# Projections, attention and output moved into one block, with single buffers and five projection banks

## The reference

```python
x = x + xattn(layernorm(x), ctx)      # 16 heads of 32, masked softmax, Wq Wk Wv Wo with biases
x = x + ffn(layernorm(x))             # fake-quantised: w_gate, w_up (1408 x 512), w_down (512 x 1408)
```

## Time and profile before

| what | value |
|---|---|
| median of three runs | 1161.38 us (1160.01 to 1163.06) |
| the profiled execution | 1157.98 us, span 1156.2 us |
| PE busy, share of the span | 92% |
| DVE, POOL, ACT busy | 66%, 55%, 44% |
| DMA queue q1 | 217.12 MB, 68.0% of 16 engines' span |
| mean granted clock of TensorE | 0.95 of full speed |

### The profile page before, as it was taken

One profiled execution on the slowest core, in us unless ns is written; L12 is line 12 of the kernel. 1 busy time (PEld: TensorE's weight loads), 2 busy tenths in 40 slices (PEclk: granted clock), 3 DMA queues, 4 the chain that ended last, 5 costly groups with the idle time before them and its releaser, 6 DMA issues. The chain is left out here.

```text
span 1156.2 us, 18186 instructions
## 1 busy us (share of the span) xinstructions
PE 1064.3 (92%) x6550; PEld 704.7 (61%) x6550; DVE 764.6 (66%) x1315; ACT 512.8 (44%) x881; POOL 630.3 (55%) x346
## 2 busy tenths in 40 slices
PE   5999999999629989999999999899995799998898
PEld 4888888888516656666666666456663344443343
DVE  5665456654329757777777777138989477877785
ACT  3322223222102657666766677641110555553553
POOL 3433455334440979999999999555434113100373
PEclk9999999999855989999999999899997799999899
DMA  6987677856699897678887774448997353100876
GB/s 205 315 266 238 212 271 255 274 167 198 203 189 189 186 233 159 149 179 177 183 185 170 160 181 115 109 137 220 286 281 190 96 224 122 36 1 2 319 243 218
DMA packets 129619, 218.08 MB, mean 189 GB/s; under 512 B 29320, under 2 KB 55688, under 8 KB 128330
## 3 DMA queue, kind: packets, MB, share of 16 engines
q1 hardware_dynamic: 129546, 217.12, 68.0%
...
## 5 line engine op out<-in xcount | busy, mean ns | idle before, releaser
L783 ACT ACTIVATE a_probs<-a_banks 128x512 f32<-128x512 f32 (+2 forms) x512 | 233.8, 535 | 128.9 <-PE a_banks L991 101.7
L718 POOL TENSOR_TENSOR a_pair_sums<-a_probs,a_probs 128x2048 f32<-128x2048 f32 x48 | 222.1, 4626 | 65.2 <-ACT a_probs L783 57.4
L858 DVE TENSOR_REDUCE a_max<-a_banks 128x2 f32<-128x512 f32 x192 | 123.2, 684 | 52.9 <-PE a_banks L962 52.7
L991 PE MATMUL a_banks<-a_queries,a_keys 97*128 97x512 f32 x384 | 147.8, 428 | 9.1 <-ACT a_probs L783 6.0
L962 PE MATMUL a_banks<-a_keys,a_queries 96*128 96x256 f32 x384 | 86.1, 320 | 32.1 <-DMA a_queries<-q_split 32.1
L967 PE MATMUL a_banks<-a_keys,a_queries 96*128 96x512 f32 (+1 forms) x256 | 115.2, 464 | 0.0
L854 DVE CUSTOM_DVE_ANT_0 a_masked_scores<-a_banks,kept_mask 128x384 f32<-128x384 f32 (+1 forms) x128 | 79.5, 621 | 49.2 <-PE a_banks L967 48.9
L858 DVE TENSOR_REDUCE a_max_parts<-a_banks 128x1 f32<-128x512 f32 x128 | 87.9, 687 | 25.1 <-PE a_banks L967 21.9
L962 PEld LDWEIGHTS a_banks<-a_keys,a_queries 96*128 96x128 f32 x384 | 70.4, 206 | 53.8 <-DMA a_queries<-q_split 32.8
L1347 POOL TENSOR_TENSOR d_out<-d_out,f_x 128x512 f32<-128x512 f32 x28 | 42.6, 1547 | 99.1 <-DVE d_out L1375 99.1
L1231 DVE SCALAR_TENSOR_TENSOR f_h<-g_up,kept_up_scales,f_h 128x512 f32<-128x512 f32 (+1 forms) x88 | 64.2, 746 | 47.2 <-ACT f_h L1196 35.4
...
## 6 DMA issues: line engine op xcount, KB each, us to landing
...
```

Of the source, the lines that this page charges most:

```text
L718: pool.tensor_tensor(PP[u % 2], PR[2 * c % 4], PR[(2 * c + 1) % 4], ALU.add).then_inc(paired, 1)
L783: act.activation(PR[kt % 4][:, j, 0:w], STB[:, n % NST, 0:w], ACT.Exp, scale=SCALE).then_inc(edone, 1)
L858: dve.tensor_reduce(out, src, AX.X, ALU.max).then_inc(wfree, 1)
L991: op = pe.matmul(out.rearrange("p (c t) -> p c t", t=SIT), keys, q, start=True, stop=True)
```

## The change

Projections, attention and output become one block. SBUF is laid out anew: buffers of the projections lie over the stacks of attention and over its probabilities and pair sums. To make room, x, context, their turned forms, and the stages of K and Q exist once or half as often (two stages for four uses a step), and the V stage holds one item in place of two. The projections keep five banks (NB = 5, PB), three serve the score pieces. Loops now run over steps 0 to 3 (EARLY = 4), steps 4 to 7 are written out.

SP loads stack 0 in step 4, stack 1 in step 5, stacks 2 and 3 and the first values in step 7, between the other transfers. The x of the next chunk is loaded after XTURN has freed x, and DVE takes its moments after the third K item and the rest of the layernorm after the fourth. The raw weights are loaded after the second V store of their own step, behind the same wait `fst`. All 56 pieces of groups 0 and 1 run two by two behind the Q and V items from the Q items of step 4 on. Eight pieces of group 2 (FIRST) come right after the first transposed scores. POOL's first pair waits for all stores of K and Q. The weights quantised last are stored from within group 0, and values 1 to 3 loaded after that.

```diff
+FIRST = 8
+S_FIRST = (2, 2, 3, 3, 3, 3, 2, 2)
...
-        NB = 8
         CHAIN_LN = 7
         HI = 4 * KT
-        TAIL = [(BATCH - 1, u) for u in range(2)]
+        TAIL = [(n // 2, n % 2) for n in range(EARLY, NCH)]
+        PB = (0, 1, 2, 6, 7)
...
-            def step(b, u, tail, final):
+            sp.wait_ge(free, NB + KT)
+            load_c(1)
+
+            def step(b, u):
                 n = 2 * b + u
-                for i in range(2):
-                    s.reach(sp, free, NB + at(n) + VALUE + 2 * i + 2)
-                    d = vs.rearrange("(n t p) c -> n p t c", t=TT, p=P)[n][:, 2 * i:2 * i + 2, :]
-                    sp.dma_start(d, VST[i][:]).then_inc(vout[i], 16)
-                if not tail:
+                late = n - EARLY if isinstance(n, int) else None
+                if late == 0:
+                    for q in sout:
+                        sp.wait_ge(q, 32 * 5)
+                for t in range(TT):
+                    s.reach(sp, free, NB + at(n) + VALUE + t + 1)
+                    sp.dma_start(vs.rearrange("(n t p) c -> n p t c", t=TT, p=P)[n][:, t, :], VST[t % 2]).then_inc(vout[t % 2], 16)
+                    if late in (0, 1):
+                        A.load_stack(sp, late, t)
+                    if t == 1:
+                        s.reach(sp, fst, 32 * (n + 1))
+                        ffn_load(n, u, b)
+                if more(n, 1):
                     s.reach(sp, free, NB + at(n) + XTURN + KT)
-                    load_c(n + 2, u)
-                    load_x(n + 2, u)
-                for i in range(4):
-                    item = KEY + 2 * i if i < 2 else query(final) + 2 * (i - 2)
-                    s.reach(sp, free, NB + at(n) + item + 2)
-                    dst = (ks, ks, qs, qs)[i]
-                    for part in range(2):
-                        d = dst[part].rearrange("(m p) t -> p m t", p=P)[:, 2 * (i % 2):2 * (i % 2) + 2, bass.ds(n * CH, CH)]
-                        sp.dma_start(d, f32(STG[i][part][:])).then_inc(sout[i], 16)
-                s.reach(sp, fq, n + 1)
-                d = gu_q[u].rearrange("(b p j) n -> b p j n", p=FP, j=FJ)[b]
-                sp.dma_start(d, FQ[:]).then_inc(fst, 16)
-                sp.dma_start(d_q.rearrange("(s p) n -> s p n", p=DP)[n], DQ).then_inc(fst, 16)
-                if not final:
-                    s.reach(sp, fst, 32 * (n + 2))
-                    ffn_load(n + 1, 1 - u, b + u)
-
-            with sp.Fori(0, BATCH - 1) as b:
+                    load_x(n + 1)
+                if late in (0, 1):
+                    for part in range(4, 6):
+                        A.load_stack(sp, late, part)
+                if late == 2:
+                    A.shift_rows(sp, 0)
+                last = not more(n, 1)
+                if last:
+                    for part in range(3):
+                        A.load_stack(sp, 2, part)
+                stage_store(n, 0)
+                if last:
+                    for part in range(3):
+                        A.load_stack(sp, 3, part)
+                stage_store(n, 1)
+                if more(n, 2):
+                    s.reach(sp, free, NB + at(n) + CTURN + KT)
+                    load_c(n + 2)
+                if last:
+                    for part in range(3, 6):
+                        A.load_stack(sp, 2, part)
+                    for q in vout:
+                        sp.wait_ge(q, 16 * (2 * NCH + 1))
+                    A.load_values(sp, 0)
+                stage_store(n, 2)
+                if last:
+                    for part in range(3, 6):
+                        A.load_stack(sp, 3, part)
+                stage_store(n, 3)
+                if not last:
+                    ffn_store(b, u)
...
+            pool.wait_ge(wlo, 3)
+            for i in range(2):
+                A.ones_row(pool, i)
+            for n in range(EARLY, NCH):
+                if more(n, 1):
+                    norm(n + 2)
+                else:
+                    pool.wait_ge(full, at(n) + XTURN + KT)
+                    for i in range(2, 4):
+                        A.ones_row(pool, i)
+                quantise_ffn(n)
+
...
-            def step(b, u, final):
+                    dve.reciprocal(FI, FC).then_inc(finv, 1)
+
+            def step(b, u):
                 n = 2 * b + u
                 for t in range(TT):
-                    if t % 2 == 0:
-                        dve.wait_ge(vout[t // 2], 16 * (n + 1))
+                    dve.wait_ge(vout[t % 2], 16 * (2 * n + t // 2 + 1))
                     dve.wait_ge(full, at(n) + VALUE + t + 1)
-                    dve.tensor_tensor(VST[t // 2][:, t % 2, :], bank(u, VALUE + t), BV[:], ALU.add).then_inc(free, 1)
+                    dve.tensor_tensor(VST[t % 2], bank(u, VALUE + t), BV, ALU.add).then_inc(free, 1)
+                    for i, k in A.early(n, t):
+                        A.largest(dve, i, k)
+                if isinstance(n, int) and n == EARLY + 2:
+                    A.rows_out(dve, 0)
                 for j in range(KT):
-                    turned(XT[u], u, n, XTURN + j, j)
-                if not final:
+                    turned(XT, u, n, XTURN + j, j)
+                if more(n, 1):
                     dve.wait_ge(lnr, n + 1)
-                    layernorm(1 - u, n + 2, b if u == 0 else b + 1)
                 for j in range(KT):
-                    staged(u, n, KEY + j, j, 0, 1, KT + j)
+                    staged(u, n, KEY + j, j, 1, KT + j)
                     ffn_rows(n, j)
-                if not final:
+                    if more(n, 1):
+                        if j == 2:
+                            moments(n + 2)
+                        if j == 3:
+                            deviations(n + 2)
+                if more(n, 1):
                     for j in range(KT):
-                        turned(CT[1 - u], u, n, CTURN + j, 2 * KT + j)
+                        turned(CT, u, n, CTURN + j, 2 * KT + j)
                 for j in range(KT):
-                    staged(u, n, query(final) + j, j, 2, 0, (2 if final else 3) * KT + j)
+                    staged(u, n, query(n) + j, j, 0, (3 if more(n, 1) else 2) * KT + j)
+                    for i, k in A.early(n, KT + j):
+                        A.largest(dve, i, k)
...
+        def early(n, item):
+
+            slot = 2 * KT * (n - EARLY) + item - KT if isinstance(n, int) else -1
+            return [divmod(2 * slot + r, NPC) for r in range(2)] if slot >= 0 else ()
...
             def pair(i, c):
                 u = 3 * i + c
                 pool.wait_ge(edone, HG * (NKT * i + 2 * c + 2))
+                if u == 0:
+                    for q in front.sout:
+                        pool.wait_ge(q, 32 * (2 * NCH + 1))
```

622 lines of the change are left out of this document (333 added, 289 removed).

## The result

The changed kernel takes 1178.78 us (median of 4 runs, 1176.87 to 1180.38) beside 1160.7 us of the kernel before (4 runs, 1157.48 to 1163.06): ratio 1.0161, 95% interval 1.0142 to 1.0181. It is slower by 18 us, twice the 9 us of the forecast, inside the range. The profiled execution took 1177.95 us with a span of 1176.2.

The account below looks back on a forecast made before the run. PE, with the raw-weights chain one us shorter, bounded the steps; the change makes that chain the limit. First pair +13.7 and stall -4.9, together +9, on 1161.4 gave 1170 us; range 1144 to 1192.

Parts of the forecast that it names:

- The chain of the weights: Steps 0 to 3: inverse, normalising, quantising, store, landing and next load of raw weights set the step, 41.4 us.
- Steps 4 to 6: Marks 3 to 6, with stacks and score pieces: distances of 45.4, 49.1 and 45.4 us.
- the late x: Steps 4 and 5: next x, queued behind weights and two stack parts, lands 3.7 us after DVE wants it.
- My upper bound of +8 for the stacks: Steps 3 to 7: at most 8 us beyond the sum if each stack part is fully in the way.
- the wait of 1.48 us: Kernel before: DVE's wait for the raw-weight load, read as agreeing that DMA completion need not be in order.
- PE's bounds: Step length PE itself allows: 37.7 us in early steps, 45.4 for marks 5 to 6 with score pieces.
- PE's pause before the Q items: Each step: PE stands still some 3.6 us before the Q items.
- The last step: Mark 7 to POOL's first pair: K and Q stores share one full queue with two stacks, 43.5 us.
- Behind it: After POOL's first pair: group 2's stall goes because stack 3 is already in place, -4.9 us.
- The clock's rival: PE's pauses lower the clock in each of seven steps, 17 us more, 1187; chance 0.15 for clock or worse.
- Loop closes sooner: Rival: raw weights are back in 6 us, a step costs 37.8, total 1149 us; chance 0.27.
- as meant: Rival: transfers overlap, steps stay at 36.3, the queue drains in step 7, total 1114 us; chance 0.08.

Follow-up runs that it names:

- e8: Changed kernel without the loads of stacks 0 and 1, filled early by ACT with other data: marks 3 to 7 take 167.2 us instead of 194.3.
- e3: Changed kernel with stack 3 loaded behind the last Q store: 1170.52 us, ratio 1.0101 to the kernel before.
- e9: Changed kernel with stack 3 behind the last Q store and the last store of quantised weights ahead of it: 1171.48 us, ratio 1.0099.
- e12: Changed kernel with stack 3 last, last weights ahead of it, group 1's row of shifts between its parts: 1174.63 us, ratio 1.0136.

## Why the prediction was right and wrong

**The chain of the weights: right, in size and cause.** 41.4 was forecast and 41.5 to 41.7 measured; a wait for the raw weights of 2.7 to 3.1 before marks 1 to 3; the quantised weights stored 27.1 after the mark (79.28 to 106.36, forecast 27.3), the load 5.0 later (4.6), the next mark 9.6 later (9.5). In the kernel before, that order alone costs 34 us. What the prediction left out is that the Q items' path is nearly as long. In steps 0 to 2 that mattered only for how to repair the chain; in steps 4 and 5 it is part of the miss.

**Steps 4 to 6: the term that failed.** "The next x stands behind the weights and two further parts and lands 3.7 after DVE wants it." The mechanism is in the rows, the size is not: DVE waited 6.96 and 6.65. The three parts of each step, taken from SP's issues after the mark and up to the next:

| | steps 0 to 2 | step 3 | step 4 | step 5 |
|---|---|---|---|---|
| mark to store of weights, forecast | 27.3 | 27.3 | 31.0 | 31.0 |
| measured | 27.1 to 27.3 | 27.1 | 34.0 | 33.9 |
| to the next load, forecast | 4.6 | 4.6 | 4.6 | 4.6 |
| measured | 5.0 | 5.3 | 5.8 | 6.7 |
| to the mark, forecast | 9.5 | 13.5 | 13.5 | 9.5 |
| measured | 9.2 to 9.6 | 14.4 | 15.4 | 10.2 |

Of the 13.4 that mark 7 is later than forecast, some 6 are the late x in two steps (DVE's wait of 7.0 and 6.7 where 3.7 was counted), 4 a later landing and 3.5 a longer way from the load to the mark (in step 5 the raw weights were there before DVE came; there the late x held the items themselves). All three go with the stacks' transfers: e8, without them, has 27 less. The late x and the slow loads lie in the queue itself, which was full. From 200 to 220 the DMA engines of the kernel after were busy throughout at 208 to 237 GB/s, and PE, DVE, ACT and POOL all but stood at the end:

```profile
200.00:205.00 5.00, 4.57 (x13) 3.64 (x14) 2.67 (x5) 0.00 (x0) 0.00 (x0) 0.66 1.03 208
...
210.00:215.00 5.00, 4.94 (x31) 4.08 (x29) 4.66 (x6) 1.38 (x2) 0.00 (x0) 1.00 1.04 237
215.00:220.00 5.00, 0.22 (x3) 0.00 (x0) 0.00 (x0) 0.00 (x0) 0.00 (x0) 0.83 1.06 228
```

The landing is another matter: it goes with how closely the last Q store stands ahead of the store of weights. Where that is 3.0 us or more it took 4.6 to 5.0, at 2.1 (step 3) 5.3, at 1.8 (step 4) 5.8, and at 0.6 (step 5) 6.7, though no part of a stack had been issued for 38 us there:

```profile
297.99 0.46 SPq L219 DMA_DIRECT2D q_split<-p_stage_lo  x1
298.56 0.82 SPq L211 DMA_DIRECT2D w_up_q<-p_gate_up_q  x1
...
305.27 0.32 SPq L204 DMA_DIRECT2D p_gate_up_raw<-in_L_ffn_w_gate_dram  x1
```

The last Q store was issued 24.0 after mark 1, but 32.2 and 33.4 after marks 4 and 5: the late x holds the fourth K item's bank, and so the Q items too. The pieces add some of it (25.4 and a landing of 5.6 in e8). I had left this path out.

I had counted the load of x at the pace of a queue with little in it, and added a part's 2.5 us only where it stood directly ahead of a transfer in program order. In a queue that is still full with what was issued earlier, everything behind is late by what is left in it. My upper bound of +8 for the stacks was passed for the same reason: it counted three more parts, and e8 measured 27 instead of the 16 in the sum.

One reading of the prediction doesn't hold either: the wait of 1.48 us shows the load of raw weights late for DVE, not transfers that complete out of order, and no row here shows that.

**PE's bounds.** 45.4 for marks 5 to 6 was too high: with 16 pieces in the step e8 needs 41.7. PE's pause before the Q items, 3.6 forecast, was 3.3, and 1.2 in step 6, where pieces stand in PE's order.

**The last step: right.** 42.7 for 43.5, with the last Q store just landed. e3 confirms the cause, a queue with stack 3 in it.

**Behind it: right in size.** The stall of 5.02 is gone, and 6.3 in all (4.9 forecast). My reason, that stack 3 was in place, is what e3, e9 and e12 support: with stack 3 late the stall is back in each.

**The clock's rival: its fall came, its price did not.** The granted clock did drop to the lower of its two levels, 1.2 GHz, after the pause (0.50 at 90 to 91 us, 1.00 from 92 on). But marks 6 to 7, at 1.00 throughout, are as far apart, 41.4, as marks 2 to 3 at 0.96: the chain hides it. "Loop closes sooner" fell with the load at 9.2 to 9.6, "as meant" with the marks.
